# A 32-expert layer: router scores ahead of the shared expert, one-hot rows by eight wide operations, output sent tile by tile

## What is computed

```
h      = rmsnorm(layernorm(x)) * norm_w              # 1024 x 256
logits = h @ router_w.T                              # 1024 x 32
scores = softmax(logits);  w, ids = top_k(scores, 4);  w = w / sum(w)
ys     = for every (token, expert) pair, grouped by expert:
         (silu(h @ w1[e][:, :128]) * (h @ w1[e][:, 128:])) @ w2[e]
routed = sum over the 4 choices of  w * ys
shared = (silu(h @ sg) * (h @ su)) @ sd              # hidden width 256
x      = x + routed + shared                         # the output
```

## Time and profile before

| what | value |
|---|---|
| median of 3 runs | 2603.31 us |
| profiled execution, its own time | 2609.1 us |
| its span, first to last instruction | 2607.3 us |
| mean granted TensorE clock | 0.885 of full speed |
| PE busy | 2143.5 us (82%) |
| DVE busy | 1653.2 us (63%) |
| ACT busy | 1054.2 us (40%) |
| POOL busy | 777.1 us (30%) |

### The profile page before, as it was taken

How to read it: one execution, slowest core, us unless ns; L and a number is a source line. 1 busy time by engine, 2 the same in 40 slices (tenths; PEclk the granted TensorE clock), 3 DMA queues, 4 the chain that set the end, 5 groups by cost and what they waited for, 6 DMA issues and landing times.

```text
span 2607.3 us, 37089 instructions
## 1 busy us (share of the span) xinstructions
PE 2143.5 (82%) x12958; PEld 1533.5 (59%) x13001; DVE 1653.2 (63%) x4280; ACT 1054.2 (40%) x2408; POOL 777.1 (30%) x1309
## 2 busy tenths in 40 slices
PE   6889965797895579975479899789999999996891
PEld 4778843564562245543146676468788788784670
DVE  4655558344466835547857888777777777764432
ACT  1223322232342324423465756245555555552230
POOL 2122223112012211110100000056666666652444
PEclk9999978897896569986569999899999999998895
DMA  6000000000000040000000000200000000005553
GB/s 238 25 17 17 1 16 1 1 2 1 1 1 26 1 173 2 1 35 1 1 0 1 1 1 1 91 1 1 5 1 5 1 1 5 7 31 187 103 138 96
DMA packets 35050, 80.55 MB, mean 31 GB/s; under 512 B 4881, under 2 KB 21777, under 8 KB 32241
## 3 DMA queue, kind: packets, MB, share of 16 engines
q1 hardware_dynamic: 30016, 65.46, 6.9%
q0 software_dynamic: 4560, 12.46, 2.3%
q10 hardware_dynamic: 288, 0.26, 0.0%
HBM read 65.71 MB, written 10.35 MB: 29 GB/s over the span
## 4 chain that ended last, share of the span: by engine, by line
PE 50%; DVE 11%; ACT 4%; issue 2%; POOL 2%; DMA 1%; POOLq 0%; SPq 0%; DVEq 0%; ACTq 0%
PE ps L2425 4%; PE ps L2394 4%; PE ps L2374 4%; PE ps L2048 4%; PE ps L2418 4%; PE ps L2067 4%; PE ps L2815 3%; PE ps L2356 2%; PE ps L2365 2%; PE ps L2357 2%; PE ps L960 2%; PE ps L2384 2%; PE ps L1000 1%; PE ps L1027 1%; DVE X L1879 1%
## 5 line engine op out<-in xcount | busy, mean ns | idle before, releaser
L2678 POOL TENSOR_TENSOR K<-K 128x512 f32<-128x512 f32 x128 | 134.3, 1049 | 182.4 <-DVE K L2469 182.4
L2096 DVE TENSOR_TENSOR_SCAN W<-W,ps 128x512 f32<-128x512 f32 x128 | 156.0, 1219 | 43.3 <-issue 25.3
L1184 ACT ACTIVATE K<-ps 128x768 f32<-128x768 f32 (+1 forms) x128 | 110.6, 864 | 165.5 <-PE ps L1000 163.6
L2048 PEld LDWEIGHTS ps<-K 128*128 128x128 f32 x1024 | 139.3, 199 | 64.6 <-issue 51.8
L2618 ACT ACTIVATE K<-ps,K 128x256 f32<-128x256 f32 x128 | 60.6, 474 | 228.4 <-DVE K L2453 228.3
L2453 DVE TENSOR_REDUCE K<-ps 128x2 f32<-128x512 f32 x128 | 87.9, 687 | 100.6 <-PE ps L2357 99.9
L2048 PE MATMUL ps<-K 128*128 128x128 f32 x1024 | 141.5, 283 | 6.8 <-DVE W L2096 6.8
L2464 DVE TENSOR_SCALAR K<-ps,K 128x128 f32<-128x128 f32 x384 | 130.7, 404 | 14.5 <-POOL K L2695 14.4
L2067 PE MATMUL ps<-W,C 128*128 128x512 f32 x256 | 133.1, 602 | 0.7 <-DVE W L2104 0.6
L2425 PE MATMUL ps<-W,K 128*128 128x256 f32 x512 | 124.4, 387 | 9.8 <-DMA K<-in_ctxT 6.2
L2374 PE MATMUL ps<-K 128*128 128x256 f32 x512 | 131.8, 380 | 0.7 <-ACT K L2637 0.7
(11 more groups left out here) (506 smaller groups left out, 5700.9 us busy)
## 6 DMA issues: line engine op xcount, KB each, us to landing
W<-in_m SPq DMA_DIRECT2D x32, 256.0 KB, 4.6
results<-K SPq DMA_DIRECT2D x63, 128.0 KB, 2.4
W<-in_wproj SPq DMA_DIRECT2D x1, 4096.0 KB, 12.4
W<-in_m SPq DMA_DIRECT2D x32, 128.0 KB, 5.8
W<-in_Wq SPq DMA_DIRECT2D x1, 2048.0 KB, 11.0
W<-in_Wo SPq DMA_DIRECT2D x1, 2048.0 KB, 15.4
W<-in_w SPq DMA_DIRECT2D x2, 1024.0 KB, 17.2
W<-K SPq DMA_DIRECT2D x4, 512.0 KB, 2.9
```

The lines of the kernel that those rows point to most:

```text
L1184: e.activation(to, made, ACT.Exp, scale=self.SCALE).then_inc(*self.up("exp"))
L2048: m = e.matmul(ps[1 + 2 * (n % 2)][:, b * 128:(b + 1) * 128], self.dtuT[h][:, i, b * 128:(b + 1) * 128], self.diag[s % 4][:, b * 128:(b + ...
L2096: e.tensor_tensor_scan(self.st[i % 3], self.a[i % 3], ps[1 + 2 * (i % 2)][:, :], 0.0, ALU.mult, ALU.add).then_inc(*sig.up("m scan"))
L2678: e.tensor_tensor(Pv, Pv, st[:, 4:6].unsqueeze(2).to_broadcast([128, 2, 256]), ALU.mult).then_inc(*sig.up("x scaled"))
```

## The change

Four edits, all in the last stage:

1. PE makes the scores of tiles 0 to 5 first, then turns tiles 6 and 7 and makes their scores. The four units of the shared hidden layer come one by one: unit (0,0) ahead of the ranks, (0,1) and (1,0) behind the ranks, (1,1) behind the one-hot products. DVE takes the largest of tiles 0 to 5 before it finishes the norm of tiles 6 and 7, and does one `shared_product` within the one-hot step and three behind the index. ACT copies the turned tiles before it issues its two stores.
2. The one-hot step is done for 8 pairs at a time: one TENSOR_TENSOR of 8 x 64 (`marks`, L2914 of the new kernel) and one of 8 x 128 (`rows`, L2917), each comparing the float16 counting row with `where` (now float16), which is repeated along the innermost direction. POOL multiplies each group's marks by the token numbers (L3093, 8 x 64, float16, in place), and makes the table `tokens` for it (L3085). Each of the 32 matmuls now waits for both.
3. SP sends each tile of x as soon as its fourth addition is done (`t final`), within the stage.
4. The last addition of a tile is not waited for by DVE any longer.

The diff, cut to its core:

```diff
@@ class L3Moe: __init__
-        self.slot, self.slots2, self.where = a.new(NT, 4, dt=I32), a.new(2, 32, dt=I32), a.new(2, 32)
+        self.slot, self.slots2, self.where = a.new(NT, 4, dt=I32), a.new(2, 32, dt=I32), a.new(2, 32, dt=F16)
-        self.hot = [(a.new(4, 128, dt=F16), a.new(4, 64, dt=F16)) for _ in range(NT)]
+        self.hot = [(a.new(8, 128, dt=F16), a.new(8, 64, dt=F16)) for _ in range(NT // 2)]
@@ sp, at its end
+        for i in range(NT):
+            d.wait_ge(sig["t final"], i + 1)
+            d.e.dma_start(g.out[i * 128:(i + 1) * 128, :], g.x(i)).then_inc(*sig.up("out", 16))
+        d.wait_ge(sig["out"], 16 * NT)
@@ pe
-        t.wait_ge(sig["r shared weights"], 48)
-        self.shared_hidden(t, 0)
-        (turns of tiles 6 and 7)
         for i in range(NT):
             if i == 6:
+                (turns of tiles 6 and 7)
                 t.wait_ge(sig["f kept"], 2)
             (scores of tile i)
-        self.shared_hidden(t, 1)
+        t.wait_ge(sig["r shared weights"], 48)
+        self.shared_hidden(t, 0, 0)
         t.wait_ge(sig["r mask"], 1)
         (ranks)
+        self.shared_hidden(t, 0, 1)
+        self.shared_hidden(t, 1, 0)
         t.wait_ge(sig["r expert"], 1)
         ...
-        for i in range(NT):
-            t.wait_ge(sig["r hot"], i + 1)
-            A, Bt = self.hot[i]
-            for k in range(4):
-                m = e.matmul(ps[6][:, 0:64], A[:, k, :], Bt[:, k, :], ...)
+        for n in range(32):
+            t.wait_ge(sig["r hot rows"], n // 8 + 1)
+            t.wait_ge(sig["r hot tiles"], n // 8 + 1)
+            A, Bt = self.hot[n // 8]
+            m = e.matmul(ps[6][:, 0:64], A[:, n % 8, :], Bt[:, n % 8, :], start=n == 0, stop=n == 31)
         m.then_inc(*sig.up("r places"))
+        self.shared_hidden(t, 1, 1)
@@ dve
-        self.shared_product(v, 0)
-        (tiles 0 to 5: copy, max, replace; tiles 6 and 7 likewise)
+        self.largest(v, 0, range(6))
+        for i in (6, 7):
+            self.norm(v, i, 3)
+        self.chosen(v, range(6))
+        self.largest(v, 1, range(6, 8))
+        self.chosen(v, range(6, 8))
         ...
-        for i in range(NT):
-            for k in range(4):
-                n = 4 * i + k
-                e.tensor_scalar(A[:, k, :], self.iota, self.where[:, 1, n:n + 1], None, ALU.is_equal)
-                m = e.tensor_scalar(Bt[:, k, :], self.iota[:, 0:64], self.where[:, 0, n:n + 1], tokid[:, i:i + 1], ALU.is_equal, ALU.mult)
-            m.then_inc(*sig.up("r hot"))
+        for c in range(4):
+            e.tensor_tensor(self.hot[c][1], self.iota[:, 0:64].rearrange("p (a n) -> p a n", a=1).to_broadcast([128, 8, 64]),
+                            self.where[:, 0, 8 * c:8 * c + 8].unsqueeze(2).to_broadcast([128, 8, 64]),
+                            ALU.is_equal).then_inc(*sig.up("r hot marks"))
+            e.tensor_tensor(self.hot[c][0], self.iota.rearrange("p (a n) -> p a n", a=1).to_broadcast([128, 8, 128]),
+                            self.where[:, 1, 8 * c:8 * c + 8].unsqueeze(2).to_broadcast([128, 8, 128]),
+                            ALU.is_equal).then_inc(*sig.up("r hot rows"))
+            if c == 0:
+                (the expert of each tile, as before) ; self.shared_product(v, 0, 0)
         ...
+        for u in range(1, 4):
+            self.shared_product(v, u // 2, u % 2)
         ...
                 m = e.scalar_tensor_tensor(g.x(i), self.G[i][:, k, :], self.gate[:, i, k:k + 1], g.x(i), ALU.mult, ALU.add)
-                v.step(m.then_inc(v.own, 1))
-                v.wait_ge(v.own, v.n)
+                if k < 3:
+                    v.step(m.then_inc(v.own, 1))
+                    v.wait_ge(v.own, v.n)
+            m.then_inc(*sig.up("t final"))
@@ pool
+        for c in range(4):
+            Bt, shape = self.hot[c][1], [128, 8, 64]
+            p.wait_ge(sig["r hot marks"], c + 1)
+            e.tensor_tensor(Bt, Bt, self.tokens[:, 8 * c:8 * c + 8].unsqueeze(2).to_broadcast(shape),
+                            ALU.mult).then_inc(*sig.up("r hot tiles"))
@@ after the last stage, SP: the eight stores of x are gone from here
```

More of the change, by code:

```diff
@@ L2859, in dve @@
         v.wait_ge(sig["w f stored"], 96)
-        for part in (0, 1, 3):
-            for i in (6, 7):
-                self.norm(v, i, part)
-        self.shared_product(v, 0)
-        v.wait_ge(sig["r consts"], 16)
+        for i in (6, 7):
+            self.norm(v, i, 0)
+        for i in (6, 7):
+            self.norm(v, i, 1)
         v.wait_ge(sig["r constants"], 3)
         C = self.consts
[L2867 to L2876, removed]
-            v.step(m.then_inc(v.own, 1))
-            v.wait_ge(v.own, v.n)
[L2879 to L2884, removed]
+        t128, ones = C[:, 136:137], C[:, 137:169]
+        self.largest(v, 0, range(6))
+        for i in (6, 7):
+            self.norm(v, i, 3)
+        self.chosen(v, range(6))
+        self.largest(v, 1, range(6, 8))
+        self.chosen(v, range(6, 8))
         e.tensor_tensor(self.mask, self.rep[:, :, 0:32], self.ext[:, :, 0:32], ALU.not_equal).then_inc(*sig.up("r mask"))
@@ L2889, in dve @@
         up, tiles, ends, begin = self.small
+        v.wait_ge(sig["r consts"], 16)
         v.wait_ge(sig["r ranks"], 1)
@@ L2985, in gates, with largest, chosen, shared_product @@
         e.nop().then_inc(*sig.up("r gates"))
-    def shared_product(self, v, c):
+    def largest(self, v, n, tiles):
         sig, e = self.sig, v.e
-        for i in range(2):
-            u = 2 * c + i
-            v.wait_ge(sig["r silu"], u + 1)
-            v.wait_ge(sig["r made"], 2 * u + 2)
-            e.tensor_tensor(self.hs[:, i, c * 512:(c + 1) * 512], self.ssh[i], self.ps[2 * i + 1][:, :], ALU.mult).then_inc(*sig.up("r shared"))
+        rows = slice(tiles[0], tiles[-1] + 1)
+        v.wait_ge(sig["r scores"], tiles[-1] + 1)
+        e.tensor_copy(self.ext[:, rows, 0:32], self.ps[7 - 2 * n][:, tiles[0] * 32:tiles[-1] * 32 + 32].rearrange("p (i x) -> p i x", x=32)
+                      ).then_inc(*sig.up("r taken"))
+        v.wait_ge(sig["r taken"], n + 1)
+        for i in tiles:
+            m = e.max(self.m8[:, i, :], self.ext[:, i, 0:32])
+        v.step(m.then_inc(v.own, 1))
+    def chosen(self, v, tiles):
+        e, rows = v.e, slice(tiles[0], tiles[-1] + 1)
+        v.wait_ge(v.own, v.n)
+        v.step(e.tensor_copy(self.sel[:, rows, 0:4], self.m8[:, rows, 0:4]).then_inc(v.own, 1))
+        v.wait_ge(v.own, v.n)
+        for i in tiles:
+            m = e.match_replace(out=self.rep[:, i, :], in_to_replace=self.sel[:, i, :], in_values=self.ext[:, i, :], imm_value=3.0e38)
+        v.step(m.then_inc(v.own, 1))
+        v.wait_ge(v.own, v.n)
+    def shared_product(self, v, c, i):
+        sig, e = self.sig, v.e
+        u = 2 * c + i
+        v.wait_ge(sig["r silu"], u + 1)
+        v.wait_ge(sig["r made"], 2 * u + 2)
+        e.tensor_tensor(self.hs[:, i, c * 512:(c + 1) * 512], self.ssh[i], self.ps[2 * i + 1][:, :], ALU.mult).then_inc(*sig.up("r shared"))
     def norm(self, v, t, part):
@@ L3022, in act @@
                          ACT.Copy).then_inc(*sig.up("f kept"))
+        for i in (6, 7):
+            a.wait_ge(sig["f normed"], i - 5)
+            e.dma_start(g.rows[i * 128:(i + 1) * 128, :], self.Y[i % 2]).then_inc(*sig.up("w f stored", 16))
         a.wait_ge(sig["r shifted"], 1)
         e.activation(self.ex, self.ex, ACT.Exp).then_inc(*sig.up("r exp"))
-        self.shared_silu(a, 1)
+        for u in range(4):
+            a.wait_ge(sig["r made"], 2 * u + 1)
+            a.wait_ge(sig["r shared"], u - 1)
+            e.activation(self.ssh[u % 2], ps[2 * (u % 2)][:, :], ACT.Silu).then_inc(*sig.up("r silu"))
         for n in range(self.TILES + 2):
@@ L3040, in act @@
                 e.activation(self.hT[j % 2], ps[4][:, 0:128], ACT.Copy).then_inc(*sig.up("t hT"))
-    def shared_silu(self, a, c):
-        sig = self.sig
-        for i in range(2):
-            u = 2 * c + i
-            a.wait_ge(sig["r made"], 2 * u + 1)
-            a.wait_ge(sig["r shared"], u - 1)
-            a.e.activation(self.ssh[i], self.ps[2 * i][:, :], ACT.Silu).then_inc(*sig.up("r silu"))
     def pool(self, p):
@@ L3278, in _ @@
             engines["sp"].wait_ge(sig["stage done"], 4 * len(stages))
-            for t in range(NT):
-                e.dma_start(out[t * 128:(t + 1) * 128, :], g.x(t)).then_inc(*sig.up("out", 16))
-            engines["sp"].wait_ge(sig["out"], 16 * NT)
+            if last < 12:
+                for t in range(NT):
+                    e.dma_start(out[t * 128:(t + 1) * 128, :], g.x(t)).then_inc(*sig.up("out", 16))
+                engines["sp"].wait_ge(sig["out"], 16 * NT)
 def kernel(**inputs):
```

57 lines of the change are left out of this document (25 added, 32 removed).

## The result

The changed kernel takes 2584.43 us (median of 6 runs, 2580.31 to 2585.82) against 2602.07 us for the kernel before in the same series (6 runs): ratio 0.9932, 95% interval 0.9917 to 0.9946, so about 17.6 us faster. The forecast was 2582.6 us and a gain of 20.7.

A forecast was written before the change was run, and what follows sets the result against it. The bound was the last stage's chain of waits: shared blocks ahead of the ranks, then DVE's one-hot instructions. Gains of 15.5 + 0 + 5.2 = 20.7 us from 2603.31 gave 2582.6, range 2580 to 2587 (2576.5 to 2590 with run spread).

The forecast's parts named there:

- Scores first: Head of the last stage: scores moved ahead of most shared work bring the ranks to DVE 16.3 us earlier, at 2383.7.
- the last score passes: PE at the stage's head: the last 8 of 32 score passes, behind the turns, take 0.9 us.
- its ends of 4.0 and 8.0: Shared unit ahead of the ranks on PE: 5.0 us taken, with 4.0 and, all slow, 8.0 as limits.
- DVE's chain from ranks to places: DVE in the stage's head: its 3.49 us from ranks to places stay, bringing the places at 2387.2.
- Wide operations: One-hot step on DVE: a group of two wide operations costs between 1.06 and 1.86 us; 1.86 taken.
- The slow end: One-hot step on DVE: 0.64 us for 512 elements and 1.22 for 1024, since one operand is repeated innermost.
- POOL excludes DVE: One-hot step: POOL's 1.05 us multiplication and DVE's operations add up rather than overlap; overlapping would save some 3 us.
- a sign of being wrong: One-hot step: the prediction called itself wrong if POOL's multiplication L3093 takes 2 us.
- a dear multiplication: Rival, one-hot step: POOL's multiplication takes 1.94 us for 512 elements, giving 2586.2 us; chance 14%.
- Cover on PE: PE behind the ranks: units (0,1) and (1,0) fit, (1,0) ending by 2395.3 to 2399.3; 24 products then catch up.
- The restart: Index cast to main loop: first turn 2.0 us late, 2.0 regained by a raised clock; net 0, ends -1 and +3.
- The end: Stage's end: stores under POOL's gathers, the stage closing on POOL's drain; 5.2 us gained, ends 0 and 7.

The follow-up runs named there:

- x6_warm: Changed kernel plus 12 unread matmuls between tile 5's scores and tile 6's turn, and 4 between the two turns, keeping PE busy; 2577.81 us, ratio 0.9918.
- x5_inner: Changed kernel with the one-hot step all on DVE and the pair index innermost in both operands; 2580.91 us, ratio 0.9929.
- x4_ondve: Changed kernel with the multiplication of the marks moved from POOL to DVE; 2584.21 us, ratio 0.9935.
- x10_again: The changed kernel run once more, unaltered, beside the kernel before; 2582.80 us, ratio 0.9931.
- x3_tail: Changed kernel with the eight output stores put back after the last stage; 2588.20 us, ratio 0.9948.
- x11_rows_inner: Changed kernel, one-hot step all on DVE, pair index innermost only in A (stationary side), PE kept busy by unread matmuls; 2575.20 us, ratio 0.9900.
- x8_mixed: Changed kernel, one-hot step all on DVE, pair index innermost only in Bt (moving side), PE kept busy by unread matmuls; 2579.72 us, ratio 0.9922.
- x7_both: Changed kernel with the edits of x5_inner and x6_warm together; 2571.92 us, ratio 0.9893.
- x12_best: x11_rows_inner with the gates spread over the main loop and the turns waiting for three shared products, not four; 2571.60 us, ratio 0.9875.

## Why the prediction was right, point by point

- **Scores first.** Right in kind, 2.3 us too much. The mis-sized terms are the last score passes (0.9 forecast, 1.91 measured), unit (0,0) (5.0 forecast, 6.03 measured) and, for 0.5 us, the last turn with its copy (1.0 forecast, 1.5 measured). I had priced the unit with a mean over a stretch in which the clock rose, and the passes and turns at the clock they had before, 1.00; here the clock was 0.50 from 2368 to 2376. x6_warm gives the first two back. The unit lay between its ends of 4.0 and 8.0; the passes had been given none.
- **DVE's chain from ranks to places.** 3.49 us moved whole (2379.01 to 2382.49).
- **Wide operations.** The slow end, 0.64 and 1.22, was measured as 0.69 and 1.22. x5_inner shows the cause.
- **POOL excludes DVE.** Right: L2914 1.53 instead of 0.68, and x4_ondve. POOL's record says 1.95 us, and the prediction had named 2 us there as a sign of being wrong. The sign was badly chosen, since the record holds the wait for DVE: 0.89 us lie behind the end of L2917, which fits about 0.9 of work (forecast 1.05), and not a dear multiplication (a rival). A full group took 2.59 (2387.93 to 2390.52), forecast 2.91. From places to cast it is 12.2 us instead of 13.7, which made up 1.5 us of what the clock had cost.
- **Cover on PE.** Right: unit (1,0) took 5.40 us, the first 24 products were done at 2392.80, and PE then waited 1.42 us for POOL.
- **The restart.** Net 0 forecast, 0.6 lost. Cast to turn takes 5.5 instead of 6.7, since unit (1,1) ran fast (3.72), and the 2.0 us of slow first passes are gone as forecast. But when DVE's gates, worked out in its fourth round, hold PE for 2.5 us, as before, the passes behind now run slow: that round takes 6.95 us from turn to turn, where it took 5.27 before, at full clock. So the two main loops are equal (133.1, 132.9), though 2.0 less was forecast: most of it was given back a few rounds later. I had not looked for this, and it is no fixed property of the kernel. In x10_again the same round takes 5.27, and instead the one from the third turn to the fourth takes 4.00 in place of 2.06, where ACT starts late:

```profile
2404.01 0.38 ACT L3052 ACTIVATE K<-ps 128x256 f32<-128x256 f32 x1 [3.49 <-remote]
```

What it waits for stays open. x4_ondve has both delays (4.07 and 6.67). That the net came within 0.6 us of the forecast is in part luck.

- **The end.** 5.2 forecast, 5.1 by the traces, 5.0 by x3_tail. POOL's drain is the bound, 2.2 us behind the last landing; what it waits for is open and no run bears on it.
- Together 20.7 forecast, 18.9 by the traces, 17.6 by the runs (14 to 22 by the interval). The mechanisms held; the clock at the stage's head was mis-sized, and a one-hot step 1.5 us shorter than forecast covered a good part of that by chance.

## What to carry to other kernels

Before pricing a step that is moved, ask at which clock it will run: behind a wait of 1.7 us on PE the passes cost 3 us more here than in x6_warm, where 16 matmuls that nobody reads fill the wait. Handing an operation with two SBUF operands to POOL was no relief for DVE: each stood while the other worked. And put a repeated operand's repetition on an outer direction: the same float16 compare took 684 ns instead of 1216. But look at who reads the result: where PE read both sides of its products at a step of 8 (x5_inner), it lost all that DVE had gained, most of it by the moving side.

## What the runs showed of the hardware that was not expected

- A product of 128 x 128 by 128 x 64 in float16 cost 0.039 us with both operands dense, 0.073 with the stationary one at a step of 8 elements, 0.121 with the moving one, 0.126 with both. (Means of one row each, in the kernel after, x11_rows_inner, x8_mixed and x5_inner.)
- The granted clock can fall while PE is busy. In x6_warm PE is busy without a gap from 2363 to 2368, and the clock goes from 0.82 to 0.50, PE being the first pair of numbers and PEclk the third from the end:

```profile
2363.00:2366.00 3.00, 3.00 (x25) 2.60 (x24) 2.10 (x10) 1.02 (x4) 2.58 (x10) 0.82 0.92 280
2366.00:2368.00 2.00, 2.00 (x10) 1.27 (x8) 1.52 (x13) 0.38 (x1) 2.00 (x6) 0.50 0.97 280
```

- A unit behind the 32 slow products of x5_inner, x7_both and x8_mixed ran slow (5.40 us), the one behind x11_rows_inner's and x12_best's ran fast (3.70).
- POOL's sequencer releases SP long after its last gather: before, that ends at 2593.90, and SP's first store is at 2601.75, 7.9 us behind, with DVE's last addition over at 2597.79. In x3_tail it is 7.9 us too (2569.59 to 2577.44), and in the kernel after it is still what SP waits for last.
